# Redrawing the hand-written issue order of all five engines in a fused two-FFN and xLSTM-attention kernel

## The reference

```python
x = x + 0.5 * ffn(layernorm(x))     # top-1 of 8 experts: relu(x@wi + lora_expert + b) @ wo + b, F = 1024
x = x + attn(layernorm(x))          # rmsnorm, q k v and gates, the scan below, @ wo, then an MLP of width 704
x = x + 0.5 * ffn(layernorm(x))     # the same weights as the first

# the scan, per head (16 heads of 16 channels), over time:
C = f * C + i * outer(v, k);  n = f * n + i * k
y = (C @ q) / max(abs(n @ q), 1)
```

## Time and profile before

| | us |
|---|---|
| median of 3 runs (932.42 to 938.03) | 936.71 |
| the profiled execution, first to last instruction | 936.9 |
| PE busy in it | 865.0 |
| DVE busy | 627.0 |
| ACT busy | 359.0 |
| POOL busy | 244.5 |

### The profile page before, as it was taken

The page is one execution under the profiler, slowest core; times in us unless marked ns, Lnnn a source line. Parts: engine busy times, 40 slices in busy tenths (PEclk is TensorE's granted clock), DMA queues, the critical chain, the costliest instruction groups (busy, mean ns, idle before and its releaser), DMA issues. The chain is left out here.

```text
span 936.9 us, 30800 instructions
## 1 busy us (share of the span) xinstructions
PE 865.0 (92%) x12744; PEld 823.7 (88%) x12744; DVE 627.0 (67%) x1502; ACT 359.0 (38%) x716; POOL 244.5 (26%) x234
## 2 busy tenths in 40 slices
PE   2958889999899998999899999999989989898998
PEld 2947869999799998999899998999979979898998
DVE  5445677585866858486676758677576787687642
ACT  4453152433533344243523436234343452233431
POOL 2013332320422313322322313332042234411110
PEclk9988999999999999999999999999999999999999
DMA  9105434212243202442133312431035035500000
GB/s 263 57 14 140 131 95 126 66 40 70 83 132 86 58 19 55 124 126 58 36 94 116 87 40 73 139 112 35 24 103 154 11 110 140 152 25 2 1 24 23
DMA packets 66313, 76.04 MB, mean 81 GB/s; under 512 B 12702, under 2 KB 48670, under 8 KB 66176
## 3 DMA queue, kind: packets, MB, share of 16 engines
q1 hardware_dynamic: 66176, 74.09, 28.2%
HBM read 56.75 MB, written 17.30 MB: 79 GB/s over the span
## 5 line engine op out<-in xcount | busy, mean ns | idle before, releaser
L644 ACT ACTIVATE r_h<-bank 128x512 fp32r<-128x512 f32 x128 | 76.5, 598 | 233.6 <-PE bank L1128 164.9
L1093 PE MATMUL bank<-xT_hi,wi_hi 128*128 128x256 f32 x512 | 148.1, 289 | 2.6 <-DVE r_l L836 1.8
L1093 PE MATMUL bank<-wo_hi,r_h 128*128 128x256 f32 x512 | 147.7, 288 | 1.1 <-DVE r_l L836 0.5
L1095 PE MATMUL bank<-xT_lo,wi_hi 128*128 128x256 f32 x512 | 144.1, 282 | 0.0
L1094 PE MATMUL bank<-xT_hi,wi_lo 128*128 128x256 f32 x512 | 144.1, 281 | 0.0
L1095 PE MATMUL bank<-wo_lo,r_h 128*128 128x256 f32 x512 | 143.7, 281 | 0.0
L1094 PE MATMUL bank<-wo_hi,r_l 128*128 128x256 f32 x512 | 143.7, 281 | 0.0
L836 DVE SCALAR_TENSOR_TENSOR r_l<-bank,r_h 128x512 fp32r<-128x512 f32 x128 | 87.9, 687 | 82.7 <-ACT r_h L644 82.1
L1093 PE MATMUL bank<-xT_hi,wgu_hi 128*128 128x256 f32 x352 | 103.1, 293 | 0.6 <-DVE gm L845 0.5
L1093 PEld LDWEIGHTS bank<-xT_hi,wi_hi 128*128 128x128 f32 x512 | 97.3, 190 | 5.0 <-DVE r_l L836 2.4
L1093 PEld LDWEIGHTS bank<-wo_hi,r_h 128*128 128x128 f32 x512 | 96.4, 188 | 3.9 <-issue 2.5
(11 more groups left out here) (157 smaller groups left out, 2143.9 us busy)
## 6 DMA issues: line engine op xcount, KB each, us to landing
dm<-f_scratch SPq DMA_DIRECT2D x128, 128.0 KB, 3.0
arena<-parts_scratch SPq DMA_DIRECT2D x96, 128.0 KB
arena<-parts_scratch SPq DMA_DIRECT2D x96, 64.0 KB
arena<-parts_scratch SPq DMA_DIRECT2D x32, 192.0 KB
x<-in_x SPq DMA_DIRECT2D x16, 256.0 KB, 3.0
parts_scratch<-pa SPq DMA_DIRECT2D x64, 64.0 KB
parts_scratch<-pb SPq DMA_DIRECT2D x64, 64.0 KB
parts_scratch<-pc SPq DMA_DIRECT2D x64, 64.0 KB
```

What stands on the lines that cost most here:

```text
L644: nc.scalar.activation(flat(r_h[:, n]), U[use % 2][:], ACT.Relu).then_inc(f_rh, 1)
L1093: nc.tensor.matmul(dst, lh, rh, start=first, stop=False, **more)
L1095: return nc.tensor.matmul(dst, lh, rl, start=False, stop=last, **more)
```

## The change

Only the five strings of `ORDER` change. Every stream has the same number of steps before and after on every engine (PE 968 letters, DVE 966, ACT 699, POOL 229, SP 271), and all instructions, buffers, sizes and waits are the same. The strings at their beginning (the rest is of the same kind):

```diff
 ORDER = {
     "PE": """
-        3G U G 5U V 2U V 2U 2V 4U V U V U 2V 2G 5U G U G 2U G U G 7U V 2U V 2U 2V 4U S U V S Y V 2U M 2V M 2S M 2Y M G 2S Y G 3U M 2U M U M Y S U S G 2Y M U G
...
+        3G U G 5U V 2U V 2U 2V 4U 2V 2U 2V 2G 6U 2G 2U G U G 6U V 4U V U 2V 2U 2S Y 3U 2V 2U 2V 2S 3M 2Y G S M Y S G 5U M S M U Y G 2U 2M S Y G Y U M G 2U G Y
...
     "DVE": """
-        2G H 3G 3H 2G 3H G H R 2H R 2H 2R H 3R G R 3H 2R H 3G 2H 3G R 2G R G R H 3R G 2R 2H R 2G R H 2R H G 2R 2H 2R D 3R D P R P Y R D G D Y 2R G Y G P Y G D
...
+        H 5G 2H G H G 4H G 3H R H 3R 3H 3R G R 3H 2R 3G H 3G R 2G 2R G 3R H R 2H G 2H R G R G 2R G 2R 2H 3R 2D 3R 2P Y R D R Y D R G D R 2G Y G P Y P Y G D G
...
     "ACT": """
-        H 6G H 2G 6H G 3H 2R 4H 3R H 2R 4H R H 6G 2H 2R 2H R 3G 3R G 2R A R Z G R G A G R G R H 2R 2A Z H G Z 8R Y 6G 3R Z R 2G 4R A 2R Y G A 3G R 2G 2R G 2R
...
+        6G 2H 2G 8H G 3H 2R 6H 6R 6H 6G 4R 2G 3R G A 3R 3G A 2G 2H R Z 2R A R G A Z 8R Y 6G R Z 5R G R A 2R G R 2G A Y 2G R 2G 2R A R G Y 3R A R Y R Z R 5G 3R
...
     "POOL": """
-        H 4G 2A G 2A Q 2W Y W Q W Y 2G W Y A W A Y 2W Y A 2Y 2G Q W G W A Y 2G W Y Q Y W G Y 2W G 2A Y G A W Y W 2Y W G Q G Q A G W Y G W Y G W G Y W A Y W A
...
+        H 4G 3A G W 2Q W A Y 2W G 2W 2Y G A Y A Y W A G W 2Y G W A 2G 2Q 2W 2Y W Y 3G Y W A W A G 2Y 2A W Y W Y W 2G W G 2Q Y 2W G Y 2G Y W 2A W 2Y G A 2W Y A
...
     "SP": """
-        H 7A F X F E C E A E A 4K E A E 2A 2K E K E K E 6A F E A K F X 2E 2A C K A K A K 2E A K E 2K E K 7A E A F K A K E F K E A E C O A K O X K A K E 2K 3E
...
+        H 6A 2F A E 2A E C K A 2K E A 2E A 3K X E 2K 2E 7A K F A 2E A F 2K X A E A C K 2E A 4K 2E 6A E A F 2A 2K E A F E C E 2K A 2O X 2E A 3K 2E K 6A K E 3A
...
```

More of the change, by code:

```diff
@@ L98 @@
[L98 to L101, removed]
@@ new lines @@
+        2M 2U Y 2U Y 2U 2V 2U M S U Y V U V Y 3U V G 3U V U 2V G 3U V U V 3U V G M 2S Y 2U G 2U V G S 2M U G 2V U Y 4U V 2U V 2U 2V 4U V U V U G 2V G 2U Y 2U
+        Y 2U 2M S M 2S G Y U S M Y G Y U M U G M 2U G 4U Y U Y V Y S V S 3M 2U Y 3U 2V 2U Y 4U 2V G 2V U G 3U M Y S 2U 2V U V G 3U G U V 2M G S 2U G 2V 5U V U
+        V 3U 2V 2U G Y 2V 4U G V U V U Y 3U Y S M U 2M S G Y 2U M S M Y G Y S U G M 2U G 3U Y 2U V Y V 3U Y U M S 2M 2V Y 2U Y 2U V 2U G U 2V U V U G 2U Y M
+        2S 2U 2V U V 2U G 2U G V 2U G 2M V G S V 5U 2V 4U 2V 2U Y G V 2U G V 2U V U V Y 4U Y U 3M G Y U 2S Y G S 2M Y U S U G M 2U G 3U Y U V U Y 3U Y V S 3M
@@ new lines @@
+        V 2U S Y M 2V 2M S U Y U Y 2U G Y M S 2U V M S M V Y U Y V Y 2M U M U Y U Y 2U 2V G V U G 5U 2V U V G 3U G U V G U V G U V 5U 2V 2U G V U V 2U G 3U V
+        G U V U G V 2U V 3U V 2U V 2U V U V 4U 2V 2U 2V""",
+    "DVE": """
+        H 5G 2H G H G 4H G 3H R H 3R 3H 3R G R 3H 2R 3G H 3G R 2G 2R G 3R H R 2H G 2H R G R G 2R G 2R 2H 3R 2D 3R 2P Y R D R Y D R G D R 2G Y P G Y P Y G D G
+        R G R G R Y G P Y 2R G R Y P D R D Y P G Y 2R Y P G Y 2R G Y R Y G 2R G 2Y 2R Y G Y R D G Y 2R Y 2G R G 4R P 4R G R 2G R G 2R G 2D 3R G Y 2R Y R G P
+        2R G 2R G Y G 2R D R G P D G P R G 3R D 2R D R G Y R G 2R G Y R G R Y R 2G R P 2Y R P Y R G R 2Y G 2R G 2R G 2Y R P 2G Y D Y R Y P D Y R D Y R G 3R Y
+        2G R P R G D 6R 3G 3R G R P Y G 3R G 3R D G 2R G R P Y R G 3R P 3G R G Y 4R 2D G R Y R 2G 3R D R G Y G 2R Y R Y G P Y 2R P Y G R 2Y G P 2R G 2R G Y G
+        Y R Y D R Y P R Y R D 2Y 2G Y 2R Y 2G R P R G D 8R Y 2G 2R Y 2G R G 3R P 2R G 4R G R G D G 2R 3G R Y R 2D G 2R P 2R 3G R G Y R G P G 4R Y R D Y 2R Y D
+        Y R Y G R 2P Y G R 2Y 2R G 2R G Y R 2D Y R G P G Y R P Y R Y G P Y 2R D Y 2G 2R G D 7R G R 3G 2R Y G P 4R G 3R G 2R G 2R G 2R 2Y D R 2G R 2G 3R 2P R D
+        Y G 2R 4G 3R Y R G D Y D 3R 2Y 2P Y 2R Y G P 2Y R G Y 2R G R Y R G D Y 2R 2D Y P R 2Y R P Y P 2R G Y 4G R G 2R 2D 3R Y 3R 2G 2R 2G R Y R G 3R G Y 2R P
+        R G 2R G 2R G 3R G R P D P R 2G D G Y 3R G R 4G R G 2R Y 2R 2Y 3R Y 2R D Y D G P 2Y G Y 2R G 2R G R Y R P Y R Y P Y R D G R P 2Y 2R Y 4G D 2R G D 3R P
+        4R 4G 4R G P D 3R G 2R 2Y 5R P 2G 3R Y R D Y G R G 2R Y G D 2R Y D P 2Y G R Y 2P Y G Y 2R Y G Y R Y G 2R D Y R 2D Y P Y G R P G 3Y 2G R G D P R Y R P
+        3Y R 2D G Y 2R Y P D Y P Y R P Y 2R D Y 3R Y D G R Y P 2R 2Y R P 2Y 2G 3R Y G R Y 2R Y 2G 4R G 2R G 4R 3G 3R G 4R G 4R G R G 2R G 2R G R 3G R G 3R G
+        2R 2G 12R""",
@@ L129 @@
+        Y W G W 2Q Y 2G 2Y G 2W 2G Y A Y 2W A 2Y G W A 2W Y G A G Q W Q 2G Y 2W 2G 2Y 2W 2A 3Y A 3W 2Y 2G W A Q G W G Y Q 3G W 2Y 2W 2A 2Y A W G W 2Y A 2G 2W
+        G W 2Q W 2Y G A W Y A Y W Y W Y A G 3W Y 2Q G A W 2Y G 2W 3Y W Y 2W 2Y 6G""",
     "SP": """
[L130 to L131 removed]
```

37 lines of the change are left out of this document (11 added, 26 removed).

## The result

| | median, us | runs | profiled span, us |
|---|---|---|---|
| before | 934.96 | 932.42 to 938.03 | 936.9 |
| after | 946.63 | 943.99 to 952.08 | 945.7 |
| ratio | 1.0128 | 95% interval 1.0082 to 1.0174 | |

I had forecast 924 and a range of 913 to 936. The time lies above the range. By the bounds of the prediction (slower is above 946.1) it is the slower side, by half a microsecond, to which I had given 0.05; no change and slower had 0.42 together.

A forecast was written before the change was run, and what follows sets the result against it. PE bounds the kernel, busy 865.0 of 936.9 us, so mainly its 71.9 us of standing can move. Gains 8.9 + 0 + 1.5 + 2.4 = 12.8 us gave 924.1, said as 924, range 913 to 936.

The forecast's parts named there:

- no change: The time stays within about 1%, between 927.3 and 946.1 us; chance 0.37.
- Step 1: Start of run 1.0: second xT_lo earlier, expert logits start 4.4 us sooner; gain 4.5 us, bounds 3.4 and 5.4.
- Step 2: V of A.0 to up1 of run 1.1: vq half 1 and an x32 start earlier; gain 1.9 us, bounds 0.8 and 2.8.
- Step 3: End of 1.1 and A.1: dn7 ends 1.6 us sooner, statistics' aggregate goes ahead of y; running gain 8.9 us.
- Step 4: Six later stretches where blocks meet: missing work 18.6 us before, 14.3 after, queues uncounted; taken as 0, bounds -4.3 and +6.
- Steps 5 and 6: Start of L.6: z goes ahead of D, gain 1.5 us; end of scan 7: z and POOL's addition move earlier, gain 2.4 us.
- step 6: End of scan 7: POOL's addition starts about 2.4 us earlier, no longer beside L.6's last r_l; gain 2.4 us.
- Taken back by new waits: Everywhere: four new hits of POOL's additions on DVE leave 4.3 us of gain, 932.5; chance 0.27 together with nothing.
- SP's queue: Six stretches: K and E issued late, D holds DVE for 3.95 us each time; 948 us, chance 0.08.
- Only the start counts double: The six stretches' 4.3 us, the rest at L.6 and a faster clock also come: 915 us; better case, chance 0.13.

The follow-up runs named there:

- e2: Order of before; POOL's additions to a block, pc, qc, wv and c_ex replaced by memsets of about the same length that read nothing: 0.9967 of before, median 932.71 us.
- e3: All engines follow before's order up to 56.5 us, then take the remaining steps in the changed order: 1.0113 of before.
- e8: Order of before, nothing left out; POOL's additions to a block in four instructions of 256 columns, qc in two: 0.9972 of before.
- experiment 6: Changed order, everything computed: POOL's addition waits for the select's end, 1.0175 of before; that with pieces and earlier table load, 1.0139; pieces and table load, 1.0021.
- e1: Changed order; POOL's additions to a block, pc, qc, wv and c_ex replaced by memsets of about the same length that read nothing: 0.9809 of before, median 920.71 us.
- e5: Changed order; only POOL's additions to a block replaced by writes that read nothing, pc, qc, wv and c_ex still read: 0.9946 of before.
- e4: All engines follow the changed order up to 58.7 us, then take the remaining steps in before's order: 1.0006 of before.
- e6: Changed order; POOL's pc, qc, wv and c_ex replaced by writes that read nothing, the additions to a block still read: 0.9940 of before.
- e7: Changed order, nothing left out; POOL's additions to a block in four instructions of 256 columns, qc in two: 1.0018 of before.
- e14: Changed order, nothing left out; additions and qc in pieces, one ACT weight piece ahead of the first normalization so the table load comes earlier: 1.0021 of before.
- e11: Changed order, nothing left out; POOL's addition in a single layer's run waits until DVE's select is done: 1.0175 of before.
- Experiments 1 and 5: First: POOL's reads replaced by writes in both orders, 0.9809 and 0.9967. Second: before's order, additions held to meet the select, 1.0285; behind it, 1.0252; meeting but not reading, 1.0092.
- e13: Order of before; POOL's addition waits for the select's first instruction, and the additions are writes that read nothing: 1.0092 of before.

## Why the prediction was wrong, by its own steps

The steps need a scale that is the same for both orders: the time at a step of PE less the PE work ahead of it, each kind of step priced at the lower quartile of its spacing in the trace of before. A smaller number is a gain. Each column is one trace. Only differences between columns are read, and none below 1 us: before, e2, e3 and e8 all begin in the old order and have `tr0` of A.0 between 54.6 and 55.5 us.

| step | before | after | before, no reads | after, no reads | gain forecast | gain without reads |
|---|---|---|---|---|---|---|
| `tr0` of A.0 | 28.4 | 30.5 | 29.3 | 25.6 | 4.5 | 3.7 |
| `up1` of 1.1 | 44.3 | 44.3 | 45.4 | 40.2 | 6.4 | 5.2 |
| `tr0` of A.1 | 50.0 | 53.2 | 50.7 | 47.0 | 8.9 | 3.7 |
| `tr0` of L.5 | 110.7 | 120.5 | 109.5 | 96.8 | 8.9 | 12.7 |
| `tr0` of L.6 | 125.4 | 136.1 | 122.0 | 109.4 | 10.4 | 12.6 |
| `tr0` of L.7 | 130.0 | 140.9 | 126.4 | 116.7 | 12.8 | 9.7 |

*Step 1, start of 1.0: right in its mechanism; the stretching and a slower PE took it.* The logits came at 15.71 instead of 18.84: 3.1 us sooner, not 4.4, since the second `xT_lo` waits for ACT's copy of its bank, which ended near 14.8, a pair of instructions that I had placed 1.3 us too early. The 0.9 us that I gave to the memsets came, the bias of the normalization is done at 6.9 and not at 7.8, but ACT's table load stood behind it (6.98 in experiment 6), so the normalization started at 8.27, before at 8.05. Then the select, 2.1 us longer, ate the lead: `u_rep` is transposed at 22.50, before at 22.77. With reads taken away it is at 20.4 and `tr0` of A.0 gains 3.7 of the 4.5.

The table shows a loss of 2.1 at `tr0` of A.0, which the select alone does not explain. Most of the rest is PE's speed. In the changed kernel its products follow each other every 0.21 us until 31.4 us, the spacing that e1's products have where the clock granted is 0.50 (below); then every 0.12 us, as before's do already from 23.4 on the earlier trace rows:

```profile
30.07 0.41 PE L1092 MATMUL bank<-xT_hi,wi_hi 128*128 128x256 f32 x1
...
32.03 0.28 PE L1092 MATMUL bank<-wo_hi,r_h 128*128 128x256 f32 x1
```

With the same start and the select not held up, PE stands 0.6 us for `u_rep` and the wide spacing ends by 19.5 us (e1, e5); with it held up PE stands 1.8 to 2.8 us and it ends at 24.4 to 31.4 (e4, e6, e7, e14 and the changed kernel). But e11 has it until 32.2 with its select free, so how much of it the select causes is not shown. By e4 and e3, the new and the old start with all reads, `tr0` of A.0 is at 55.0 and 55.4: even, not 2.1 apart.

*Step 2, V of A.0:* 1.5 more (5.2 - 3.7) against 1.9 forecast. Right, without reads. In the changed kernel `up1` of 1.1 starts at 85.3, as in the earlier trace rows.

*Step 3, end of 1.1 and A.1: wrong even without reads.* I wrote of y and a P that they "now sit before the bias that waits for that power anyway". These are the rows of after without reads that answer to the earlier trace rows:

```profile
107.29 0.36 DVE L941 BATCH_NORM_AGGREGATE a_mv<-a_st 128x2 f32<-128x6 f32 x4
108.00 1.64 POOL L541 TENSOR_TENSOR a_rs<-a_ve,minus_half 128x8 f32<-128x8 f32 x1 [4.70 <-DVE a_ve L945]
108.97 0.41 PE L1319 MATMUL bank<-vq,pt 128*32 128x34 f32 x26 [2.10 <-issue]
109.70 0.18 DVE L1068 TENSOR_SCALAR den<-bank 128x16 f32<-128x16 f32 x1 [1.78 <-PE bank L1338]
111.35 0.15 DVE L948 SCALAR_TENSOR_TENSOR a_nb<-a_mv,a_rs 128x8 f32<-128x8 f32 x1
```

The power was done at 109.64; the bias that uses it was issued at 111.35, behind y, which waited 1.78 us for PE's Mc, and the P. DVE's string had a wait on PE in it that I had not priced. The step loses 1.5 instead of gaining 2.5.

*Step 4, the six stretches: mis-sized at nothing.* I had counted 4.3 us less missing work and took 0. Without reads, from A.1 to L.5, the gain is 12.7 - 3.7 = 9.0. With reads the same stretch loses (120.5 - 110.7) - (53.2 - 50.0) = 6.6. The count pointed the right way, and 9.0 is twice what it counted. What overturned it, POOL's and DVE's moved steps costed at nothing beyond their place, had a bound of only 6 us of loss.

*Steps 5 and 6.* The wait for z at L.6 is gone in the new order, and the `r_l` of the earlier trace rows is 0.43 us, as forecast. But without reads the lead falls from 12.6 to 9.7 at the end, where I had added 3.9. In the changed kernel D and SP had a part here: S of block 7 waits 2.15 us for `arena` at 799.2. Part of the 2.9 us after L.6 without reads is PE's clock, the third number from the end in these rows of e1:

```profile
786.00:790.00 4.00, 3.63 (x153) 3.09 (x154) 1.70 (x4) 1.59 (x4) 3.77 (x9) 0.50 0.31 71
790.00:796.00 6.00, 4.66 (x32) 4.43 (x30) 1.03 (x4) 0.81 (x2) 0.50 (x2) 0.51 0.82 238
```

PE had stood 2.66 us for the normalization of L.6 just before 786.37, and 12 products take 2.56 us (from 792.57) instead of 1.40. In e2 the clock is 1.00 from 797 to 850, the same steps. The rest is not settled.

**The step that failed** is the treatment of the exclusion: the sum priced every moved POOL and DVE step at its usual duration. I saw the exclusion once in the trace of before, 2.1 us, and took its removal as a gain in step 6 (the same trace has a second such hit, `fg` at 465.22, 2.15 us instead of 0.24 beside an addition). As a risk I gave it to one rival, as four new hits by the additions alone, and 932.5. There were 26 more stretched instructions, 22.1 us more of stretching, and four other kinds of POOL instruction that do the same at 0.3 to 1.1 us a time. The reads cost the change 22 us more than they cost before by the medians (25.9 less 3.8) and 27 by the ratios; with them the forecast's own 12.8 gives 936.9 - 12.8 + 22 = 946, or 951. What stands ahead of the prediction says that the engines wait for each other on semaphores only. That is not so here: this wait has no semaphore, and the profile shows it as a longer instruction. The Trainium skill (SBUF — State Buffer, who interferes with whom) states that a DVE instruction with two SBUF inputs contends with a GpSimd instruction that reads SBUF and not with one that only writes it. Experiments 1 and 5 agree with both halves: the same instruction at the same place costs 2.1 us as a reader and nothing as a writer.

That the sum without reads came out near the forecast, 12.8 against 12.0 by the medians (9.4 in the profiles, 15 by the ratios), is in good part luck. Steps 1 and 2 gave 5.2 of 6.4; step 3 lost 1.5 where I had a gain of 2.5; step 4 gave 9.0 where I had nothing; and after L.5 3.0 were lost where I had added 3.9.

**The rivals.** "Taken back by new waits" had the mechanism and a third of its size (its 936.9 - 4.3 is 932.6, not 932.5). "SP's queue" had the time, 948, and the wrong mechanism: D's waits for its DMA sum to 3.4 us in three (before 4.0 in one), `arena` adds 3.9. "Only the start counts double" had a gain of 21.9 us; the order by itself gave 9 to 15.

## What to carry to other kernels

When an order is redrawn and no instruction changes, compare each engine's busy time first. If it moved, something holds instructions up, and waits and queues are the second question. Before the change, list which instructions can lock each other out and lay the two engines' strings beside each other in time; what is hit by chance 9 times in 1,500 instructions before may be hit 35 times after. The order of before holds such misses without anybody having written them down; whether by tuning or by chance no run shows. Shorter locking instructions helped in both orders (by 0.011 and 0.003); a guard by semaphore on an engine with an in-order queue can cost more than what it prevents (0.9% in e13, where the additions read nothing).

## What the runs showed of the hardware that I had not expected

An exclusion is paid by tiny instructions in full: 0.19 us became 2.28 (and 3.12 instead of 1.22 for D), for as long as the addition on POOL lasted. Splitting POOL's instruction lets DVE in between the pieces.

Two kinds of DVE instruction with one SBUF input were held up too, both `tensor_scalar`: `fg` and `g_ve` (0.17 us, once 0.85 beside an addition). Line 893 of the changed kernel, minimum, median and maximum, and the moment at 249 us beside a `pc` that ends at 249.87:

```profile
L893 DVE TENSOR_SCALAR fg<-fg x8: 176/184/981, 73.8 to 772.2; 128x64 f32<-128x64 f32 x8
...
248.71 1.16 POOL L555 TENSOR_TENSOR pc<-gm,pb 128x512 bf16<-128x512 f32 x1 [1.81 <-ACT pb L764]
249.28 0.64 DVE L893 TENSOR_SCALAR fg<-fg 128x64 f32<-128x64 f32 x1
```

The same page of the Trainium skill lists `tensor_scalar` among the operations that can take the shared port pair in a two-port mode; the reduction, which it says never contends, never did here (185 to 189 ns in 16).

And `fg` is held up by an instruction of POOL that only writes. All that is left of the stretching in e1 and e2 is `fg`, once and three times, each time beside a memset; in e1:

```profile
L902 DVE TENSOR_SCALAR fg<-fg x8: 177/183/570, 68.3 to 746.4; 128x64 f32<-128x64 f32 x8
...
236.23 1.11 POOL L521 MEMSET pc<- 128x512 bf16 x2 [1.83 <-ACT pb L773]
236.82 0.57 DVE L902 TENSOR_SCALAR fg<-fg 128x64 f32<-128x64 f32 x1
```

The two memsets run until 237.34, and `fg` ends at 237.39. So taking the reads away frees the instructions with two SBUF inputs, not this one.

The exclusion works both ways: POOL's `wv`, 0.65 us, took up to 1.57 when a D was under way, and 24 of POOL's instructions were stretched by 16.9 us in the changed kernel against 13 by 7.4 before. In e1 what is left of POOL's own is 3.5 us in 6. Of the 24.5 us of span between after and e1, 6.8 lie within PE's busy time. That these are due to the reads is not shown: e3, with all reads and nearly the same stretching (28.7 us), has PE busy for 855.4 us, less than e1's 857.1, at a mean granted clock of 0.985 against 0.977 in after.
